# Edge stage of a graph layer: split parts side by side in one product, and a new order of work on VectorE

## The reference, cut to what matters

```python
xn = layernorm(x)
r = concat([xn[src], xn[dst], edge_attr]) @ Wr.T + br
q = (xn @ Wq.T + bq).reshape(n, H, D)
k = (r @ Wk.T + bk).reshape(e, H, D)
v = (r @ Wv.T + bv).reshape(e, H, D)
a = einsum('ehd,ehd->eh', q[dst], k) / sqrt(D)
amax = segment_max(a, dst)
ae = exp(a - amax[dst])
asum = segment_sum(ae, dst)
out = segment_sum(v * (ae / asum[dst])[..., None], dst)
```

## Time and profile before

| | us |
|---|---|
| median of 3 runs | 1856.7 |
| lowest, highest run | 1849.52, 1867.2 |
| profiled execution, own time | 1861.11 |
| its span, first to last instruction | 1859.4 |

### The profile page before, as it was taken

How to read it: one execution, slowest core, us unless ns; L and a number is a source line. 1 busy time by engine, 2 the same in 40 slices (tenths; PEclk the granted TensorE clock), 3 DMA queues, 4 the chain that set the end, 5 groups by cost and what they waited for, 6 DMA issues and landing times. The chain is left out here.

```text
span 1859.4 us, 26827 instructions
## 1 busy us (share of the span) xinstructions
PE 1625.0 (87%) x7160; PEld 1189.9 (64%) x7162; DVE 1301.8 (70%) x3259; ACT 1026.1 (55%) x3674; POOL 698.6 (38%) x723
## 2 busy tenths in 40 slices
PE   7989979999999999999999999999992777888523
PEld 6867767777777777777777777777772333444311
DVE  5875728788877888778878788788774445332688
ACT  3982225777677776777677776777664334200011
POOL 0001224555555555555555555555542000000033
PEclk9989989999999999999999999999996788999855
DMA  5664327566656666566665666566652433000001
GB/s 179 204 224 157 123 87 229 190 203 205 220 196 191 207 209 220 192 198 206 220 207 193 207 211 223 195 208 208 203 181 101 142 102 136 0 1 1 23 12 44
DMA packets 129671, 300.29 MB, mean 162 GB/s; under 512 B 29088, under 2 KB 50727, under 8 KB 129522
## 3 DMA queue, kind: packets, MB, share of 16 engines
q0 software_dynamic: 63600, 180.17, 28.7%
q1 hardware_dynamic: 60738, 107.59, 18.7%
q10 hardware_dynamic: 5184, 10.81, 1.5%
HBM read 271.40 MB, written 66.58 MB: 182 GB/s over the span
## 5 line engine op out<-in xcount | busy, mean ns | idle before, releaser
L1193 ACT ACTIVATE wv<-vv,expd 128x64 f32<-128x64 f32 x1256 | 315.2, 333 | 0.0
L1205 ACT ACTIVATE old<-old,expd 128x64 f32<-128x64 f32 x1256 | 307.8, 333 | 0.0
L1140 POOL DMA_INDIRECT merge<-new,put_id x157 | 159.9, 1019 | 374.5 <-DVE new L1357 341.3
L1401 PE MATMUL psK<-M_hi,efT_hi 128*128 128x512 f32 x628 | 253.2, 403 | 6.3 <-ACT efT_hi L1166 6.3
L1401 PE MATMUL psV<-M_hi,efT_hi 128*128 128x512 f32 x628 | 255.8, 407 | 0.0
L1402 PE MATMUL psK<-M_lo,efT_hi 128*128 128x512 f32 x628 | 249.5, 397 | 0.0
L1402 PE MATMUL psV<-M_lo,efT_hi 128*128 128x512 f32 x628 | 249.5, 397 | 0.0
L1314 DVE TENSOR_TENSOR wv_lo<-wv,wv_hi 128x512 fp32r<-128x512 f32 x157 | 108.9, 693 | 196.2 <-ACT wv_hi L1198 190.5
L1111 POOL DMA_INDIRECT kv<-kv_table,src_id x157 | 164.3, 1047 | 74.9 <-issue 30.8
L1182 ACT ACTIVATE expd<-diff 128x32 f32<-128x32 f32 (+1 forms) x79 | 18.1, 229 | 310.4 <-DVE diff L1338 310.4
L1111 POOL DMA_INDIRECT qc<-q_table,dst_id x157 | 155.4, 990 | 53.7 <-issue 46.9
(11 more groups left out here) (271 smaller groups left out, 3310.1 us busy)
## 6 DMA issues: line engine op xcount, KB each, us to landing
efT<-in_ef_turned_dram SPq DMA_DIRECT2D x78, 512.0 KB, 6.7
merge<-empty ACTq DMA_DIRECT2D x4, 2640.0 KB, 9.7
rows<-merge SPq DMA_DIRECT2D x40, 264.0 KB, 3.5
row_block<-dst_rows POOLq DMA_DIRECT2D x13, 768.0 KB, 5.9
dst_line<-dst_rows SPq DMA_DIRECT2D x78, 128.0 KB, 3.5
end_line<-end_rows SPq DMA_DIRECT2D x78, 128.0 KB, 5.3
kv_table<-kv_out SPq DMA_DIRECT2D x10, 512.0 KB, 3.3
raw<-in_L_gnn_Wr_dram SPq DMA_DIRECT2D x12, 256.0 KB, 5.4
```

Of the source, the lines that this page charges most:

```text
L1140: pool.indirect_dma_start(out=merge[2 * (p % 2) + u][:, :], out_offset=bass.IndirectOffsetOnAxis(ap=put_id[:, t:t + 1], axis=0), in_=new[p ...
L1193: act.activation(wv[:, u, h * DH:(h + 1) * DH], vv[p % 2][:, u, h * DH:(h + 1) * DH], ACT.Copy, scale=expd[p % 2][:, u, 0, h:h + 1]).then_ ...
L1205: act.activation(rows, rows, ACT.Copy, scale=expd[p % 2][:, u, 1, h:h + 1]).then_inc(old_scaled, 1)
L1401: pe.matmul(out[:, :], efT_hi[b][:, u, c, :], Me_hi[:, c, col:col + D], start=c == 0, stop=False)
```

## The change

Two parts.

**One product in place of two.** The high and low parts of the exponentials become one tile `exp_parts` [P, 2, 2, H], those of the runs one tile `run_parts`. A single matmul with 16 moving columns gives both partial results side by side in PSUM, and the two halves are added on VectorE by a `tensor_reduce` each: `top_sum` ahead of the new maximum, `sum_den` between the two row additions of `merge_rows`.

**Another order.** On ScalarE the copy to the high part of the exponentials (`weights_high`) stands behind `weigh_v` of the same pair instead of ahead of it. On VectorE the second addition of values, the one-hots and the scan come ahead of the low parts; the second low part of the weighted tile stands between the scores of the pair's two tiles.

```diff
--- before.py
+++ after.py
@@ -1017,25 +1017,25 @@
         score_hi = sb("score_hi", [P, 2, H], F32R)
         score_lo = sb("score_lo", [P, 2, H], F32R)
         runs = sb("runs", [H, 2 * P])
-        runs_hi = sb("runs_hi", [P, 2, H], F32R)
-        runs_lo = sb("runs_lo", [P, 2, H], F32R)
+        run_parts = sb("run_parts", [P, 2, 2, H], F32R)
+        top_sum = sb("top_sum", [P, 2, H])
         diff = two("diff", [P, 2, 2, H])
         expd = two("expd", [P, 2, 2, H])
-        exp_hi = two("exp_hi", [P, 2, H], F32R)
-        exp_lo = two("exp_lo", [P, 2, H], F32R)
+        exp_parts = two("exp_parts", [P, 2, 2, H], F32R)
         vv = two("vv", [P, 2, D])
         wv = sb("wv", [P, 2, D])
         wv_hi = sb("wv_hi", [P, 2, D], F32R)
         wv_lo = sb("wv_lo", [P, 2, D], F32R)
...
+        sum_den = sb("sum_den", [P, 2, H])
...
         sorted_s = psO[0:H, 0:2 * P]
-        den = psO[:, 2 * P:2 * P + 2 * H].rearrange("p (u h) -> p u h", h=H)
+        den = psO[:, 2 * P:2 * P + 4 * H].rearrange("p (u s h) -> p u s h", s=2, h=H)
         turned_s = psT[:, 0:2 * H].rearrange("p (u h) -> p u h", h=H)
-        top = psT[:, 2 * H:4 * H].rearrange("p (u h) -> p u h", h=H)
+        top = psT[:, 2 * H:6 * H].rearrange("p (u s h) -> p u s h", s=2, h=H)
 
...
+        def top_at(p):
+
+            return 4 * p + 1
+
         def newmax_at(p):
+            return 4 * p + 2
+
+        def diff_at(p):
+            return 4 * p + 4
+
+        def scaled_at(p):
 
             return 3 * p + 1
 
-        def diff_at(p):
+        def summed_at(p):
+            return 3 * p + 2
+
+        def den_at(p):
             return 3 * p + 3
-
-        def scaled_at(p):
-
-            return 2 * p + 1
-
-        def den_at(p):
-            return 2 * p + 2
 
         def exp_at(p):
 
@@ -1170,7 +1176,7 @@
                 act.wait_ge(runs_turned, 2 * p + n)
                 if p >= 1:
                     act.wait_ge(top_done, 2 * p)
-                act.activation(runs_hi[:, 0:n, :], turned_s[:, 0:n, :], ACT.Copy).then_inc(runs_copied, 1)
+                act.activation(run_parts[:, 0:n, 0, :], turned_s[:, 0:n, :], ACT.Copy).then_inc(runs_copied, 1)
 
             def weights(p):
                 n = tiles_of(p)
@@ -1180,8 +1186,11 @@
                     act.wait_ge(den_step, scaled_at(p - 2))
                     act.wait_ge(exp_low, p - 1)
                 act.activation(expd[p % 2][:, 0:n, :, :], diff[p % 2][:, 0:n, :, :], ACT.Exp, scale=SCALE).then_inc(exp_ready, 1)
+
+            def weights_high(p):
+                n = tiles_of(p)
                 act.wait_ge(exp_ready, exp_at(p))
-                act.activation(exp_hi[p % 2][:, 0:n, :], expd[p % 2][:, 0:n, 0, :], ACT.Copy).then_inc(exp_ready, 1)
+                act.activation(exp_parts[p % 2][:, 0:n, 0, :], expd[p % 2][:, 0:n, 0, :], ACT.Copy).then_inc(exp_ready, 1)
 
             def weigh_v(t):
                 p, u = t // 2, t % 2
...
                     weigh_v(2 * p - 2)
+                    weights_high(p - 1)
 
...
+            def scores(t):
+                add_k(t)
+                times_q(t)
+                sum_scores(t)
+
             def split_scores(p):
                 b, n = p % 2, tiles_of(p)
                 dve.wait_ge(score_step, score_at(2 * p + n - 1))
@@ -1287,7 +1302,7 @@
                 dve.wait_ge(runs_copied, p + 1)
                 if p >= 1:
                     dve.wait_ge(top_done, 2 * p)
-                dve.tensor_tensor(runs_lo[:, 0:n, :], turned_s[:, 0:n, :], runs_hi[:, 0:n, :].bitcast(F32),
+                dve.tensor_tensor(run_parts[:, 0:n, 1, :], turned_s[:, 0:n, :], run_parts[:, 0:n, 0, :].bitcast(F32),
                                   ALU.subtract).then_inc(runs_low, 1)
 
             def exp_low_part(p):
...
-                dve.tensor_tensor(exp_lo[b][:, 0:n, :], expd[b][:, 0:n, 0, :], exp_hi[b][:, 0:n, :].bitcast(F32),
+                dve.tensor_tensor(exp_parts[b][:, 0:n, 1, :], expd[b][:, 0:n, 0, :], exp_parts[b][:, 0:n, 0, :].bitcast(F32),
                                   ALU.subtract).then_inc(exp_low, 1)
 
...
@@ -1328,7 +1343,10 @@
                 dve.wait_ge(old_in[b], landed(p))
                 if p >= 2:
                     dve.wait_ge(put[b], landed(p - 2))
-                dve.tensor_tensor(new[b][:, 0:n, ROW:TROW], old[b][:, 0:n, ROW:TROW], top[:, 0:n, :],
+                dve.tensor_reduce(top_sum[:, 0:n, :], top[:, 0:n, :, :].rearrange("p u s h -> p u h s"),
+                                  AX.X, ALU.add).then_inc(max_step, 1)
+                dve.wait_ge(max_step, top_at(p))
+                dve.tensor_tensor(new[b][:, 0:n, ROW:TROW], old[b][:, 0:n, ROW:TROW], top_sum[:, 0:n, :],
                                   ALU.max).then_inc(max_step, 1)
                 dve.wait_ge(max_step, newmax_at(p))
                 if p >= 2:
@@ -1351,10 +1369,13 @@
                 for u in range(n):
                     t = 2 * p + u
                     dve.wait_ge(summed, t + 1)
+                    if u == n - 1:
+                        dve.tensor_reduce(sum_den[:, 0:n, :], den[:, 0:n, :, :].rearrange("p u s h -> p u h s"),
+                                          AX.X, ALU.add).then_inc(den_step, 1)
                     dve.wait_ge(old_scaled, H * (t + 1))
                     dve.tensor_tensor(new[b][:, u, 0:D], psS[u][:, :], old[b][:, u, 0:D], ALU.add).then_inc(new_ready, 1)
-                dve.wait_ge(den_step, scaled_at(p))
-                dve.tensor_tensor(new[b][:, 0:n, D:ROW], den[:, 0:n, :], old_den[:, 0:n, :], ALU.add).then_inc(den_step, 1)
+                dve.wait_ge(den_step, summed_at(p))
+                dve.tensor_tensor(new[b][:, 0:n, D:ROW], sum_den[:, 0:n, :], old_den[:, 0:n, :], ALU.add).then_inc(den_step, 1)
 
             dve.memset(kk[:, :, :, DH:HW], 1.0).then_inc(ones_placed, 1)
             dve.wait_ge(ones_placed, 1)
@@ -1363,21 +1384,20 @@
                 here, last, older = p < PAIRS, 1 <= p <= PAIRS, p >= 2
                 if last:
                     add_v(2 * p - 2)
-                if older:
-                    exp_low_part(p - 2)
-                    wv_low_part(2 * p - 4)
                 if last and tiles_of(p - 1) == 2:
                     add_v(2 * p - 1)
                 if last:
                     row_one_hots(p - 1)
                     scan(p - 1)
+                if older:
+                    exp_low_part(p - 2)
+                    wv_low_part(2 * p - 4)
+                if here:
+                    scores(2 * p)
                 if older and tiles_of(p - 2) == 2:
                     wv_low_part(2 * p - 3)
-                if here:
-                    for t in range(2 * p, 2 * p + tiles_of(p)):
-                        add_k(t)
-                        times_q(t)
-                        sum_scores(t)
+                if here and tiles_of(p) == 2:
+                    scores(2 * p + 1)
                 if last:
                     runs_low_part(p - 1)
                 if here:
...
-                    pe.matmul(top[:, u, :], from_end[:, u, :], runs_hi[:, u, :], start=True, stop=False)
-                    pe.matmul(top[:, u, :], from_end[:, u, :], runs_lo[:, u, :], start=False, stop=True).then_inc(top_done, 1)
+                    pe.matmul(top[:, u, :, :], from_end[:, u, :], run_parts[:, u, :, :], start=True, stop=True).then_inc(top_done, 1)
 
...
-                    pe.matmul(den[:, u, :], same[p % 2][:, u, :], exp_hi[p % 2][:, u, :], start=True, stop=False)
-                    pe.matmul(den[:, u, :], same[p % 2][:, u, :], exp_lo[p % 2][:, u, :], start=False, stop=True)
+                    pe.matmul(den[:, u, :, :], same[p % 2][:, u, :], exp_parts[p % 2][:, u, :, :], start=True, stop=True)
                     pe.matmul(psS[u][:, :], same[p % 2][:, u, :], wv_hi[:, u, :], start=True, stop=False)
                     pe.matmul(psS[u][:, :], same[p % 2][:, u, :], wv_lo[:, u, :], start=False, stop=True).then_inc(summed, 1)
```

## The result

The changed kernel takes 1869.07 us (median of 20 runs, 1865.46 to 1872.53), the kernel before, timed beside it, 1856.05 (20 runs, 1849.52 to 1870.13). The ratio is 1.006, 95% interval 1.0043 to 1.0077 (the two medians alone give 1.007): slower by 0.6%, small but clear of noise, and within the 1% that I had called no change. 1866 was forecast. Note the spread: the kernel before ranges over 20.6 us, the changed one over 7.1.

What follows compares the result with a forecast made beforehand. The prediction took a ring of ScalarE and VectorE, 14.2 us a round, as the bound: 1861.1 + 25 (reductions) - 18 (earlier loads) = 1868, less 2 for the profiled execution: 1866 us, range 1842 to 1886.

Steps and rivals of the forecast that it cites:

- the ring: ScalarE from expd to runs_hi, then VectorE from runs_lo to the second diff: claimed as the bound, 14.2 us a round.
- TensorE at 87% busy: Claimed close but with room, waiting for runs_hi each round; the rival that it bounds: 1830 us, chance 0.07.
- TensorE's idle piece ahead of the maxima's product: Sign in the profile after: TensorE's idle time at this place was to grow to over 1 us a round.
- A reading: Clock case: from 510 to 585 us TensorE was said to idle 1.1 us in each of five rounds.
- the clock: TensorE's granted clock, 1.00 before; the case that it falls to its lower level for long had chance 0.02.
- The two reductions: sum_den and top_sum on VectorE behind runs_lo: 0.32 us a round, +25 us over 78 rounds.
- The new order gains nothing on the ring: VectorE's wait for wv_hi moves to runs_lo, 1.9 us of it, with 0.7 for the exponentials; no gain.
- The loads: SyncE's dst_line and efT go out 3.3 us earlier, old lands about 2 us sooner: -18 us, bounds 8 and 20.
- the waits for `old`: VectorE's waits ahead of the maximum for the gather of old, making rounds longer: 20 us too much in 75 rounds.
- The first rival: Early loads delay the gather of qc, so old lands no sooner: 1878, up to 1886; 0.24 together with reductions at upper bound.
- The sum: Whole kernel: 1861.1 + 25 - 18 = 1868 against the profiled execution, less 2: 1866 us, 0.5% above 1856.7.
- the 2 us subtracted for the place of the profiled execution: Profiled execution was 4.4 us above the runs' median, part likely the wait for old; 2 us of it subtracted.

Runs made afterwards that it cites:

- e6: The changed kernel with ScalarE's copy of the runs' high part moved ahead of the scaling of the old rows: 1773.31 us, ratio 0.9549.
- e1: The kernel before with only the new order on VectorE and ScalarE; split tiles, two matmuls each, no reductions: 1844.88 us, ratio 0.9935.
- e3: e1 with one more wait in SyncE's queue, holding a round's loads back about as late as in the kernel before: 1864.4 us, ratio 1.0022.
- e11: The kernel before with four buffers instead of two for the rows of indices, so all four loads go out earlier: 1840.99 us, ratio 0.9922.

## Why the prediction was right

*What bounds the kernel.* Right. The ring of 10.47 us of ScalarE and VectorE's stretch is there in the changed kernel with the same ScalarE part, and moving a step of 1.14 us out of it shortened the median round by 1.13. TensorE at 87% busy is no bound: four matmuls more a round changed nothing, until the ring was opened. Its room is that between the two bounds: 14.55 us a round against the 13.28 of e6, so 1.27 us.

One sign of the prediction failed: TensorE's idle piece ahead of the maxima's product is 37.8 / 71 = 0.53 us on average, not over 1. The prediction put all of TensorE's room in that place. The waits of the weight loads show that it is spread: 66.9 us lie there and 41.4 ahead of the product that sorts the scores. A reading was wrong, too: from 510 to 585 us TensorE idled 75.00 - 71.75 = 3.25 us in five rounds, 0.65 each and not 1.1. Neither enters the sum; the clock stayed at 1.00, as forecast.

*The two reductions.* Sized at 0.10 and 0.22 us; 0.10 and 0.22 measured. The 0.02 for the longer read had no row of its own and came out within 0.01. The round grew by 0.34 instead of 0.32, so 27 us instead of 25; the rest is 0.02 in the dependent steps behind. Against e1, the pair of products with its reductions costs 1869.1 - 1844.9 = 24 us by the medians, and 1867.8 - 1840.4 = 27 us by the spans of the two profiled executions.

*The new order gains nothing on the ring.* Right. The wait went to the low part of the runs, 1.91 us of it, where 1.9 was said; 0.74 for the exponentials, where 0.7 was said. With the order alone the round is the old floor of 14.21 us.

*The loads.* Sized at -18 us; the waits for `old` fell from 20 us to 2 in the profiled executions. In the medians they are worth less, 12 us in e1. The place, 3.3 us earlier, and the cause are shown from both sides: held back, the waits return under the new order; moved ahead, they vanish under the old one. I had expected `old` to land about 2 us sooner, and it is 1.8. But the way is another: the transfer itself is 3 us shorter, and its issue is 1.2 us later by GpSimd's wait for the scatter, which the prediction did not name. That the two come out near the 2 us is in part luck.

The first rival was right that early loads delay something ahead of `old`, and it missed the scatter. The scatter's median landing is 3.4 us in e1 against 2.3 in e3, where only the loads were held back. The gather of `qc` lands in 5.4 us in the median in the changed kernel and in 3.5 in e11, where the loads go out ahead of it. The trace of the kernel before has no landing for `qc`, so what it lost by the change is not shown. The Trainium skill, DMA: Bandwidth & Descriptors, section Queues, rings and completion order, has each DMA engine take turns between the queue rows with work, packet by packet. The longer landings beside the loads agree with it; no run here shows the turns themselves. The delay is smaller than the gain.

*The sum.* 1866 against 1869.07. Two terms were off by 2 us each: the reductions (27, not 25) and the 2 us subtracted for the place of the profiled execution. With both mended the sum is 1861.1 + 27 - 18 = 1870, against 1869.53 for the profiled execution after. The guess behind it, that the waits for `old` vary from run to run, agrees with the ranges of 20.6 and 7.1 us over 20 runs each, but no experiment was made for it. It would mean that the median run before had some 14 us of these waits to lose and not 18: 1856.05 + 27 - 1869.07.

## What to carry to other kernels

When two engines close a ring, a wait on one of them is no reserve until it is known at which tie the ring hangs: filling the wait at one tie moved it to the next, and only steps taken out of the stretch between the two ties shortened the round. Saving work on an engine that waits is worth nothing yet, and what it costs elsewhere is worth its full price: the same merge of products lost 24 us here and won 34 us once the ring was open. Where an engine's list is reordered, look at which loads hang on its steps: all that this change gained came by a queue whose list the diff doesn't touch.

## What was not expected of the hardware

One load of 512 KB issued 6.3 us behind the exponentials made the gather of `old`, issued 0.5 us later, take 6.6 us in the median; with that load issued 8 us earlier, the gather took 4.4 us. The first row has all gathers of `old` in the kernel before, the second in the run with three buffers:

```profile
DMA to landing us min/median/max: 3.3/6.6/8.8
```
```profile
DMA to landing us min/median/max: 3.4/4.4/7.8
```

And the same loads in the gap behind the scatter raised the scatter's own landing from a median of 2.3 us to 3.4 in e1, though the scatter is the same. The rows are the kernel before, e1, and e3, which is e1 with the loads held back:

```profile
DMA to landing us min/median/max: 2.2/2.3/3.5
```
```profile
DMA to landing us min/median/max: 2.2/3.4/6.8
```
```profile
DMA to landing us min/median/max: 2.2/2.3/3.3
```
